# Sums of squares of a graph kernel by block transpose, row sums and small DMAs in place of a product with ones

## The chip, the core and the metric

The kernel runs on one core of a Trainium2 chip. The core has a matrix engine (TensorE, PE in the profile), a vector engine (VectorE, DVE), a scalar engine (ScalarE, ACT), GpSimd (POOL) and SyncE (SP), which here issues all DMAs. Each engine works through its own list of instructions in order, and semaphores hold an instruction back until another engine has done its part. The metric is the device time of one execution in microseconds; lower is better.

## What is computed

128 graphs of 128 nodes with 256 features pass through four layers. Each layer is a graph network with a residual and a layer norm behind it: `x = layernorm(x + layer(x, adj))`. The change lies in the first layer, a hypergraph convolution with a hidden width of 512 and a layer norm of its own over that width:

```python
h = relu(hypergraph_conv(x, adj, W1, b1))
h = layer_norm(h, gamma, beta)          # mean and variance over 512 columns
y = hypergraph_conv(h, adj, W2, b2)
return y + x
...
x = _layernorm(x + _L0_gnn_ref(...))    # then three more layers of this form
```

The variance of the hidden row of a node is its mean of squares less its squared mean. The hidden state is held with the 512 hidden columns along partitions (four chunks of 128) and the nodes along the free axis, so the sum of squares of one node runs over partitions.

## The kernel before

Two graphs make a pair, and 64 pairs are worked off. A pair passes through some forty steps on five engines, and the steps of several pairs are interleaved: a written-out start (`fill`), a loop over `n` from 7 to 61 (`FIRST, LAST = 7, 62`, 55 passes), and a written-out end (`drain`). Each engine has its own `body(n)` that lists its steps in a fixed order. A pass of the loop works on pair `n` in the first steps, on `n-1` in the hidden layer, on `n-2` in the second layer, and so on to `n-5`.

TensorE's pass (`body`, lines 784 to 823) runs `R` (first product of the hidden layer, two halves), `G`, `xT` (transpose of `x1`, the first layer's output, of pair `n-2`), `H2W`, `Ax2`, `XAB`, `H1`, `AP3`, `P` (product of the hidden state with W2 for pair `n-1`), `squares`, `Tr`, `AXB`, `H1W`, `Ax3`, `Gx`, `H2`, `GP` (the product with `p`, which ends layer one of pair `n-1`), `TK`. Products in full precision are split into high and low halves; the low half (`..._lo`) is made by VectorE or GpSimd from a high half (`..._hi`) that ScalarE writes.

The sum of squares of pair `n-1` goes this way. ScalarE squares the hidden state (`square_r`, L1044), GpSimd adds the four chunks to one (`add_squares` L221, `sum_squares` L227, tile `sq1`), and TensorE sums over partitions by two products with a column of ones (`squares`); each fp32 product shows as two matmuls. The result lies in PSUM beside `P`. ScalarE squares the mean (`square_mean` L1091), VectorE makes the variance (`wide_var` L1699 and L1702), ScalarE the root (`root_h` L1095), VectorE the reciprocal and `p` (`make_p` L1709, L1717), ScalarE its high half (`round_p`, `p_hi`), GpSimd its low half (`low_p`, `p_lo`), and TensorE runs `GP`. Behind `GP` VectorE adds the residual (`sum_n1` L1750) and takes moments (`moments(n1)` L1575, L1584), ScalarE the root (`root(n1)` L1005), and VectorE makes `x1` in the next pass (`make_x1` L1595, L1613), which TensorE's `xT` reads.

SP's pass issues the loads of pair `n+2` (`reload`) and the store of pair `n-5`, which waits for the last layer norm. No other DMA runs in the loop.

Of the kernel before, what the change touches and what calls it, by code (L numbers as in the profile page):

```python
# [46 lines left out]
def build(nc, x, adjT, w1T, w2T, wab, v1, v2, v3, wk, columns, rows, eye, out):  # L47
# [5 lines left out]
    with ExitStack() as ctx:  # L53
        def sb(name, shape, dt=F32):
            return ctx.enter_context(nc.sbuf_tensor(name, [C, *shape], dt))
# [4 lines left out]
        def sem(name):  # L60
            return ctx.enter_context(nc.semaphore(name))
# [33 lines left out]
        sq, sq2, sq1 = sb("sq", [KH, 2, C]), sb("sq2", [2, 2, C]), sb("sq1", [2, C])  # L95
        h_mean2 = sb("h_mean2", [2])
        h_veps, h_std, h_rstd = sb("h_veps", [2]), sb("h_std", [2]), sb("h_rstd", [2])
        p_f, p_s = sb("p_f", [2, D]), hi_lo("p", [2, D])
# [25 lines left out]
        class Norm:  # L124
# [13 lines left out]
            def mv(self, p):  # L138
# [11 lines left out]
        table_loaded = sem("table_loaded")  # L150
        consts_step, beta_made, w1_hi, w1_lo, w2_scaled, w2_mean, w2_centred, w2c_hi, w2c_lo = (
            sem(s) for s in ("consts_step", "beta_made", "w1_hi", "w1_lo", "w2_scaled", "w2_mean",
                             "w2_centred", "w2c_hi", "w2c_lo"))
        betaW_made, wab_hi, wab_lo, v_hi, v_lo, b2_made = (
# [5 lines left out]
            sem(s) for s in ("ht_made", "ht_counted", "be_max", "be_made", "be_hi", "be_lo", "bh_high", "bh_made"))  # L160
        dn_0, dn_1, dn_2, dn_3, gl_made, gd_made = (sem(s) for s in ("dn_0", "dn_1", "dn_2", "dn_3", "gl_made", "gd_made"))
# [3 lines left out]
        sq_made, sq_half, sq_sum = sem("sq_made"), sem("sq_half"), sem("sq_sum")  # L165
        hm2, hv, hve, hstd, hrstd = (sem(s) for s in ("h_mean2", "h_var", "h_veps", "h_std", "h_rstd"))
        deg_max, deg_inv = sem("deg_max"), sem("deg_inv")
        p_made, p_hi, p_lo, xb_made = sem("p_made"), sem("p_hi"), sem("p_lo"), sem("xb_made")
# [21 lines left out]
        def bank(stage, pair):  # L190

            return BANK_OF.get((stage, pair), BANK[stage])

        def inputs(p):
# [94 lines left out]
        def _(sp):  # L289
# [80 lines left out]
        def _(pe):  # L370
# [68 lines left out]
            def P(p, h):  # L439
                if p == 0 and h == 0:  # L440
                    pe.wait_ge(w2c_lo, 1)
# [154 lines left out]
            def fill():  # L596
# [10 lines left out]
                pe.wait_ge(gt_hi, 1)  # L607
                pe.wait_ge(w2_mean, 1)
                G(2)
# [174 lines left out]
            def body(n):  # L784
# [22 lines left out]
                P(n - 1, 1)  # L807
                squares(n - 1)
                pe.wait_ge(ax2_lo, n - 2)
# [179 lines left out]
        def _(act):  # L989
# [212 lines left out]
            def round_w2():  # L1202
                act.wait_ge(w2_centred, 1)
                copy(w2c_s[0][:, :, 0:D], w2g[:]).then_inc(w2c_hi, 1)

# [178 lines left out]
            def body(n):  # L1384
# [178 lines left out]
        def _(dve):  # L1563
# [90 lines left out]
            def scale_G(p):  # L1654
# [3 lines left out]
                dve.wait_ge(pe_did["G"], upto(p))  # L1658
                dve.tensor_reduce(dn, psum[:, both, 2 * C:2 * C + 2], AX_X, ALU.add).then_inc(dn_0, 1)
                dve.wait_ge(dn_0, upto(p))  # L1660
                dve.tensor_scalar(dn_max[:], dn, TINY, None, ALU.max).then_inc(dn_1, 1)
                dve.wait_ge(dn_1, upto(p))
                dve.reciprocal(dn_inv[:], dn_max[:]).then_inc(dn_2, 1)
                dve.wait_ge(dn_2, upto(p))
                dve.scalar_tensor_tensor(out=dinv[:], in0=dn, scalar=0.0, in1=dn_inv[:],
                                         op0=ALU.is_gt, op1=ALU.mult).then_inc(dn_3, 1)
                dve.wait_ge(dn_3, upto(p))
                if begun(p - 1):
# [18 lines left out]
            def invert_edges(p):  # L1687
# [5 lines left out]
                dve.reciprocal(be_inv[:], be[:]).then_inc(be_made, 1)  # L1693

            def wide_var(p):
                b = bank("P", p)
                h_var = psum[:, b:b + 2, D + 4]
                dve.wait_ge(hm2, upto(p))
                dve.scalar_tensor_tensor(out=h_var, in0=psum[:, b:b + 2, D + 2], scalar=1.0 / DH,  # L1699
                                         in1=h_mean2[:], op0=ALU.mult, op1=ALU.subtract).then_inc(hv, 1)  # L1700
# [21 lines left out]
            def node_degree(p):  # L1722
                b = bank("AXB", p)
                dve.wait_ge(pe_did["AXB"], upto(p))
                dve.tensor_scalar(degm[:], psum[:, b:b + 2, D], DEG_EPS, None, ALU.max).then_inc(deg_max, 1)
                dve.wait_ge(deg_max, upto(p))
                dve.reciprocal(rdeg[:], degm[:]).then_inc(deg_inv, 1)

            def make_agg(p):
                b = bank("AXB", p)  # L1730
                dve.wait_ge(xa_out, upto(p))
                dve.wait_ge(deg_inv, upto(p))
                for g in range(2):
# [36 lines left out]
            def mean_w2():  # L1770
                dve.wait_ge(pe_did["W2"], 1)
                dve.tensor_scalar(w2mean[:], psum[:, bank("W2", 0), 0:D], 1.0 / DH, None, ALU.mult).then_inc(w2_mean, 1)

            def centre_w2():
                dve.wait_ge(w2_mean, 1)
                dve.wait_ge(w2_scaled, KH)
                dve.tensor_tensor(w2g[:], w2g[:], bc(w2mean[:], [C, KH, D], 1), ALU.subtract).then_inc(w2_centred, 1)

            def high_w2():
                dve.wait_ge(w2_centred, 1)  # L1780
                dve.tensor_copy(w2c_s[0][:, :, 0:D], w2g[:]).then_inc(w2c_hi, 1)

            def low_w2():
                dve.wait_ge(w2c_hi, 1)
                dve.tensor_tensor(w2c_s[1][:, :, 0:D], w2g[:], f(w2c_s[0][:, :, 0:D]),  # L1785
                                  ALU.subtract).then_inc(w2c_lo, 1)

# [198 lines left out]
            def body(n):  # L1986
# [203 lines left out]
        def _(pool):  # L2190
# [121 lines left out]
            def body(n):  # L2312
# [98 lines left out]
```

## Time and profile before

| | us |
|---|---|
| median of three runs | 1393.92 (1392.55 to 1394.46) |
| the profiled execution, device time | 1393.31 |
| its span, first to last instruction | 1391.2 |
| outside the span | 2.1 |

Busy time of the span: TensorE 99%, VectorE 82%, ScalarE 81%, GpSimd 72%; DMA engines a tenth. The chain of work that ended last lies on TensorE for 98% of the span. The granted TensorE clock is 0.997 of full speed on the mean. Times in the rows below are microseconds from the start of the span, if no ns stands beside them; a matmul's end is modelled and matmuls overlap, so the cost of a group of them is read from start to start.

### The profile page before, as it was taken

To read this page: it belongs to the slowest core of one execution; us is meant where nothing else is said; L and a number is where in the kernel's file an instruction comes from. 1 tells how busy PE (TensorE), PEld (TensorE's weight loads), DVE (VectorE), ACT (ScalarE), POOL (GpSimd) and SP (SyncE) were. 2 spreads that over 40 slices of the span, in tenths; PEclk is the share of its full clock that TensorE was granted. 3 is DMA by queue.
4 is the path that set the end of the run, shared out by engine and by line. 5 is a ranking of instruction groups with operands and counts; after the bars stand their busy time and mean duration, and the time that the engine had idled before them with its cause. 6 is when DMAs were issued, how large, how long until landed. Compare 5 with 4: busy or idle time off the path is not lost.

```text
span 1391.2 us, 35333 instructions
## 1 busy us (share of the span) xinstructions
PE 1376.9 (99%) x10946; PEld 1335.9 (96%) x10946; DVE 1134.6 (82%) x4092; ACT 1122.7 (81%) x2639; POOL 1003.6 (72%) x1059
## 2 busy tenths in 40 slices
PE   8999999999999999999999999999999999999997
PEld 8999999999999999999999999999999999999996
DVE  7888788888887887788888878878888888888896
ACT  6777887887888878878878888888788788887776
POOL 5758778778778787787787787777877877877531
PEclk9999999999999999999999999999999999999999
DMA  4100110110100101101101101011011011010000
GB/s 143 36 20 20 40 39 20 39 40 20 39 29 31 39 21 39 39 20 40 39 20 40 32 28 39 21 39 39 21 39 39 20 40 37 23 40 21 8 22 34
DMA packets 29961, 47.17 MB, mean 34 GB/s; under 512 B 3408, under 2 KB 12240, under 8 KB 29776
## 3 DMA queue, kind: packets, MB, share of 16 engines
q1 hardware_dynamic: 29776, 44.91, 10.1%
q8 instruction: 90, 1.47, 0.4%
q14 instruction: 95, 0.78, 0.2%
HBM read 28.12 MB, written 16.78 MB: 32 GB/s over the span
## 4 chain that ended last, share of the span: by engine, by line
PE 98%; ACT 1%; issue 0%; DVE 0%; DMA 0%; SPq 0%; ACTq 0%; DVEq 0%
PE psum L374 95%; PE psum L473 2%; PE psum L417 1%; DMA n_s<-w2T_in 0%; ACT x L1010 0%; ACT tk L1172 0%; ACT h_hi L991 0%; DVE w2c_lo L1785 0%; DVE w2g L1767 0%; ACT w2c_hi L991 0%; ACT r_f L1015 0%; SPq L291 0%; ACT h_f L1015 0%; DVE n_st L1575 0%; DVE n_s L260 0%
## 5 line engine op out<-in xcount | busy, mean ns | idle before, releaser
L208 POOL TENSOR_TENSOR h_lo<-h_f,h_hi 128x512 fp32r<-128x512 f32 x120 | 154.9, 1291 | 93.6 <-ACT h_hi L991 93.4
L1010 ACT ACTIVATE x<-n_s,n_shift,n_rstd 128x256 f32<-128x256 f32 x384 | 208.0, 590 | 4.2 <-DVE n_shift L1599 4.1
L215 POOL TENSOR_TENSOR r_lo<-r_f,r_hi 128x512 fp32r<-128x512 f32 x123 | 158.7, 1292 | 44.1 <-ACT r_hi L991 43.9
L2229 POOL TENSOR_TENSOR n_s<-tk,mask 128x512 f32<-128x512 f32 x60 | 62.5, 1041 | 154.1 <-DVE mask L1652 133.0
L1575 DVE BATCH_NORM_STATS2 n_st<-n_s 128x6 f32<-128x256 f32 x384 | 141.9, 412 | 2.2
L374 PE MATMUL psum<-v_hi,h_hi 128*128 128x256 f32 x512 | 137.8, 292 | 2.0 <-ACT h_hi L991 2.0
L374 PE MATMUL psum<-A_f,x 128*128 128x128 f32 x1024 | 135.5, 275 | 0.6 <-ACT x L1010 0.5
L1015 ACT ACTIVATE h_f<-psum,columns 128x256 f32<-128x256 f32 x256 | 107.6, 472 | 34.8 <-PE psum L374 34.7
L374 PE MATMUL psum<-v_lo,h_hi 128*128 128x256 f32 x512 | 133.3, 282 | 0.0
L374 PE MATMUL psum<-gx_hi,w1T_hi 128*128 128x256 f32 x512 | 132.3, 281 | 0.0
L374 PE MATMUL psum<-gx_hi,w1T_lo 128*128 128x256 f32 x512 | 131.9, 281 | 0.0
L374 PE MATMUL psum<-w2c_hi,r_hi 128*128 128x258 f32 x512 | 129.5, 284 | 0.8 <-DVE w2c_lo L1785 0.8
L374 PE MATMUL psum<-w2c_lo,r_hi 128*128 128x258 f32 x512 | 129.4, 283 | 0.0
L374 PEld LDWEIGHTS psum<-A_f,x 128*128 128x128 f32 x1024 | 124.6, 191 | 1.6 <-ACT x L1010 1.1
L1005 ACT ACTIVATE n_std<-psum,eps_c 128x2 f32<-128x2 f32 x165 | 42.2, 256 | 93.5 <-DVE psum L1584 93.5
L208 DVE TENSOR_TENSOR ax_lo<-psum,ax_hi 128x512 fp32r<-128x512 f32 x128 | 88.5, 692 | 24.3 <-ACT ax_hi L991 21.1
L374 PE MATMUL psum<-wab_hi,x1T_hi 128*128 128x512 f32 x256 | 105.8, 413 | 0.0
L1015 ACT ACTIVATE r_f<-psum,columns 128x256 f32<-128x256 f32 x256 | 100.3, 469 | 5.9 <-PE psum L374 5.0
L374 PE MATMUL psum<-v_hi,h_lo 128*128 128x256 f32 x512 | 102.1, 281 | 0.0
L374 PE MATMUL psum<-gx_lo,w1T_hi 128*128 128x256 f32 x512 | 101.8, 281 | 0.0
L374 PE MATMUL psum<-wab_lo,x1T_hi 128*128 128x512 f32 x256 | 100.9, 394 | 0.0
L208 DVE TENSOR_TENSOR x1T_lo<-psum,x1T_hi 128x512 fp32r<-128x512 f32 x64 | 44.2, 691 | 69.3 <-ACT x1T_hi L991 69.3
(173 smaller groups left out, 5200.1 us busy)
## 6 DMA issues: line engine op xcount, KB each, us to landing
x_in<-x_in_dram SPq DMA_DIRECT2D x64, 256.0 KB, 2.8
out<-x SPq DMA_DIRECT2D x64, 256.0 KB, 2.0
at_in<-adjT SPq DMA_DIRECT2D x64, 128.0 KB, 2.2
x<-v_in SPq DMA_DIRECT2D x3, 256.0 KB, 5.7
n_s<-w2T_in SPq DMA_DIRECT2D x2, 256.0 KB, 3.3
r_f<-w1T_in SPq DMA_DIRECT2D x2, 256.0 KB, 5.1
h_f<-wab_in SPq DMA_DIRECT2D x2, 256.0 KB, 5.6
rows<-rows_in SPq DMA_DIRECT2D x1, 256.0 KB, 6.0
```

The lines of the kernel that those rows point to most:

```text
L208: return e.tensor_tensor(dst[1][:], src, f(dst[0][:]), ALU.subtract).then_inc(signal, 1)
L215: e.tensor_tensor(r_s[1][:, half], r_f[:, half], f(r_s[0][:, half]), ALU.subtract).then_inc(r_lo[h], 1)
L374: return pe.matmul(o, a, b, start=start, stop=stop)
L417: last = pe.transpose(psum[:, bank("Tr", p), cols(g)], Gd[:, g, :], ident[:])
L473: last = pe.transpose(psum[:, bank("xT", p), (2 * m + g) * C:(2 * m + g + 1) * C], x1[p % 2][:, g, cols(m)], ident[:])
L1005: act.activation(nm.std[:], nm.mv(p)[:, :, 1], ACT.Sqrt, bias=eps_c[:, 0:1]).then_inc(nm.rooted, 1)
L1010: last = act.activation(dst[:, g, :], nm.s[:, g, :], ACT.Identity, scale=nm.rstd[:, g:g + 1], bias=nm.shift[:, g:g + 1])
L1015: return act.activation(dst[:, m].rearrange("p g c -> p (g c)"), psum[:, bank(stage, p), (m % 2) * 2 * C:(m % 2 + 1) * 2 * C], ACT.Relu, b ...
L1575: last = dve.bn_stats(nm.st[:, g, :], sum_in_psum(p, g) if nm is n1 else nm.s[:, g, :])
L2229: pool.tensor_tensor(n4.s[:], tk[:], bc(mask[:], [C, 2, D], 2), ALU.mult).then_inc(tk_masked, 1)
```

## The change

In the 55 passes of the loop, the two products with ones are gone, and the sum over partitions is made in four steps: VectorE transposes the 32x32 blocks of `sq1` (`turn_squares`), sums each row of 32 to a partial sum (128x8 values), SP writes these to a small DRAM tensor with four DMAs of 128 runs of 8 bytes each, waits for them, and reads them back with one DMA of 128 rows of 32 bytes (`move_squares`); VectorE adds the four partial sums of each node (`fold_columns`). `wide_var` then reads the sum from SBUF. Pairs outside the loop keep the products with ones.

The orders change with it. TensorE runs `TK` ahead of `GP`. VectorE has `turn_squares` behind `invert_edges`, and `fold_columns` and `wide_var` stand behind `make_agg`, `make_p` behind `sum_n2`. ScalarE has `copy_h1w` ahead of `root_h`, and `high_ax3` between `root_h` and `round_p`. GpSimd has `low_GT`, `make_xb` and `make_x2c` ahead of `low_p`. SP has `move_squares` between `reload` and `store`. Several semaphores are merged into one that counts steps (`w2_step`, `dn_step`, `deg_step`); the waits stay where they were. The core of the diff:

```diff
+        sq_rows = nc.dram_tensor("sq_rows", (C, 4, 2), F32, kind="Internal").ap()
...
         def sum_squares(e, p):
             e.wait_ge(sq_half, upto(p))
             if begun(p - 1):
                 e.wait_ge(pe_did["P"], upto(p - 1))
+            if in_loop(p - 1, 1):
+                e.wait_ge(sq_turned, by_dma(p - 1))
...
+            def move_squares(p):
+                sp.wait_ge(sq_folded, by_dma(p))
+                if in_loop(p - 1, 1):
+                    sp.wait_ge(sq_moved, 16 * by_dma(p - 1))
+                for a in range(4):
+                    sp.dma_start(sq_rows.rearrange("(b i) a g -> a i b g", b=4)[a],
+                                 sq_part[32 * a:32 * a + 32]).then_inc(sq_stored, 16)
+                sp.wait_ge(sq_stored, 64 * by_dma(p))
+                if in_loop(p - 1, 1):
+                    sp.wait_ge(sq_added, by_dma(p - 1))
+                sp.dma_start(sq_cols[:], sq_rows).then_inc(sq_moved, 16)
...
                 if n + 2 < NP:
                     reload(n + 2)
+                if n < LAST:
+                    move_squares(n - 1)
                 store(n - 5)
...
-                    late(o, terms, 1, stop=h == 1)
+                    last = late(o, terms, 1, stop=h == 1)
+                if h == 1 and in_loop(p, 1):
+                    last.then_inc(pe_did["P"], 1)
...
                 P(n - 1, 1)
-                squares(n - 1)
                 pe.wait_ge(ax2_lo, n - 2)
...
                 H2(n - 3)
+                pe.wait_ge(n2.summed, n - 1)
+                TK(n - 4)
                 pe.wait_ge(p_made, n)
                 GP(n - 1)
-                pe.wait_ge(n2.summed, n - 1)
-                TK(n - 4)
...
                 copy_GT(n)
-                root_h(n - 1)
                 round_GT(n)
                 make_x3(n - 4)
+                copy_h1w(n - 3)
+                root_h(n - 1)
+                high_ax3(n - 4)
                 round_p(n - 1)
-                copy_h1w(n - 3)
-                high_ax3(n - 4)
                 high_gx(n)
...
+            def turn_squares(p):
+                dve.wait_ge(sq_sum, upto(p))
...
+                dve.transpose(sq_t[:].rearrange("p g c -> p (g c)"), sq1[:].rearrange("p g c -> p (g c)")).then_inc(sq_turned, 1)
+                dve.wait_ge(sq_turned, by_dma(p))
...
+                dve.tensor_reduce(sq_part[:].rearrange("p b g -> p g b"),
+                                  sq_t[:].rearrange("p g (b j) -> p g b j", b=4), AX_X, ALU.add).then_inc(sq_folded, 1)
+
+            def fold_columns(p):
+                dve.wait_ge(sq_moved, 16 * by_dma(p))
...
+                dve.tensor_reduce(h_sq[:], sq_cols[:].rearrange("p a g -> p g a"), AX_X, ALU.add).then_inc(sq_added, 1)
...
                     invert_edges(n + 1)
+                turn_squares(n - 1)
                 low_xbw(n - 2)
...
-                wide_var(n - 1)
-                make_p(n - 1)
                 node_degree(n - 2)
                 make_agg(n - 2)
+                fold_columns(n - 1)
+                wide_var(n - 1)
                 sum_n2(n - 2)
+                make_p(n - 1)
                 low_ax3(n - 4)
...
+                low_GT(n)
                 make_xb(pool, n - 1)
-                low_GT(n)
+                make_x2c(n - 3)
                 low_p(pool, n - 1)
-                make_x2c(n - 3)
                 low_h2(pool, n - 3)
```

## Rows read from the trace of the kernel before

**Rows 1.** The page's first part: busy us, share, instructions of each engine.
```profile
PE 1376.9 (99%) x10946; PEld 1335.9 (96%) x10946; DVE 1134.6 (82%) x4092; ACT 1122.7 (81%) x2639; POOL 1003.6 (72%) x1059
```

**Rows 2.** Two stretches: length, busy us of each engine, granted clock, DMA share, GB/s.
```profile
170.00:1350.00 1180.00, 1179.94 (x9443) 1148.10 (x9443) 965.48 (x3503) 965.03 (x2270) 885.34 (x925) 1.00 0.10 31
...
1370.00:1380.00 10.00, 7.96 (x63) 7.38 (x62) 8.33 (x36) 6.88 (x16) 0.20 (x1) 1.00 0.08 28
```

**Rows 3.** Chain that ended last, first and last such piece: start, length, work.
```profile
99.80 10.49 PE psum L374 x78
...
1267.60 10.49 PE psum L374 x78
```

**Rows 4.** TensorE in order of time, the products with ones: start, length, work.
```profile
704.40 0.50 PE L374 MATMUL psum<-ones,sq 128*128 128x1 f32 x4
704.76 0.42 PE L417 MATMUL psum<-ident,Gd 128*128 128x128 f32 x2
```

**Rows 5.** DMA issues of the page: KB each, median us to landing.
```profile
x_in<-x_in_dram SPq DMA_DIRECT2D x64, 256.0 KB, 2.8
out<-x SPq DMA_DIRECT2D x64, 256.0 KB, 2.0
...
columns<-columns_in SPq DMA_DIRECT2D x1, 8.0 KB, 1.8
```

**Rows 6.** SP's queue in order of time, one pass's loads being issued.
```profile
713.28 0.33 SPq L291 DMA_DIRECT2D at_in<-adjT  x1
713.66 0.44 SPq L294 DMA_DIRECT2D x_in<-x_in_dram  x1
```

**Rows 7.** VectorE in order of time, from the edge counts to the sum of n2.
```profile
699.88 0.28 DVE L1683 TENSOR_SCALAR HT<-at_in 128x256 fp32r<-128x256 f32 x1
700.20 0.42 DVE L1685 TENSOR_REDUCE ht_count<-HT 128x2 f32<-128x256 f32 x1
...
700.95 0.69 DVE L1640 TENSOR_TENSOR xbw_lo<-psum,xbw_hi 128x512 fp32r<-128x512 f32 x1
...
705.14 0.17 DVE L1699 SCALAR_TENSOR_TENSOR psum<-psum,h_mean 128x2 f32<-128x2 f32 x1
...
705.98 0.88 DVE L1717 SCALAR_TENSOR_TENSOR p_f<-psum,h_rstd,betaW 128x256 f32<-128x256 f32 x2
706.77 0.15 DVE L1725 TENSOR_SCALAR degm<-psum 128x2 f32<-128x2 f32 x1
...
708.14 0.69 DVE L1744 SCALAR_TENSOR_TENSOR n_s<-psum,x 128x512 f32<-128x512 f32 x1
```

**Rows 8.** ScalarE in order of time: p's high half, root of n1, squares.
```profile
706.90 0.62 ACT L991 ACTIVATE p_hi<-p_f 128x512 fp32r<-128x512 f32 x1
...
712.70 0.29 ACT L1005 ACTIVATE n_std<-n_mv,eps_c 128x2 f32<-128x2 f32 x1
...
718.57 1.06 ACT L1044 ACTIVATE sq<-r_f 128x1024 f32<-128x1024 f32 x1
```

**Rows 9.** GpSimd in order of time: p's low half, the last sum of squares.
```profile
707.59 1.28 POOL L208 TENSOR_TENSOR p_lo<-p_f,p_hi 128x512 fp32r<-128x512 f32 x1
...
721.08 0.89 POOL L227 TENSOR_TENSOR sq<-sq 128x256 f32<-128x256 f32 x1
```

**Rows 10.** TensorE in order of time: last matmul of GP, start of R, xT.
```profile
710.43 0.28 PE L374 MATMUL psum<-p_lo,GT_hi 128*128 128x256 f32 x1
...
711.96 0.28 PE L374 MATMUL psum<-gx_hi,w1T_hi 128*128 128x256 f32 x1
...
715.02 0.60 PE L473 MATMUL psum<-ident,x 128*128 128x128 f32 x4
```

**Rows 11.** VectorE in order of time, behind GP: sum of n1, moments, x1.
```profile
710.91 0.67 DVE L1750 SCALAR_TENSOR_TENSOR psum<-xb,psum 128x512 f32<-128x512 f32 x1
...
712.51 0.15 DVE L1584 BATCH_NORM_AGGREGATE n_mv<-n_st 128x2 f32<-128x6 f32 x1
...
713.33 0.99 DVE L1613 TENSOR_SCALAR x<-psum,n_mv,n_rstd 128x256 f32<-128x256 f32 x2
```

More of the change, by code:

```diff
@@ L150, in build @@
         table_loaded = sem("table_loaded")
-        consts_step, beta_made, w1_hi, w1_lo, w2_scaled, w2_mean, w2_centred, w2c_hi, w2c_lo = (
-            sem(s) for s in ("consts_step", "beta_made", "w1_hi", "w1_lo", "w2_scaled", "w2_mean",
-                             "w2_centred", "w2c_hi", "w2c_lo"))
+        consts_step, beta_made, w1_hi, w1_lo, w2_scaled, w2_step = (
+            sem(s) for s in ("consts_step", "beta_made", "w1_hi", "w1_lo", "w2_scaled", "w2_step"))
         betaW_made, wab_hi, wab_lo, v_hi, v_lo, b2_made = (
@@ L160, in build @@
             sem(s) for s in ("ht_made", "ht_counted", "be_max", "be_made", "be_hi", "be_lo", "bh_high", "bh_made"))
-        dn_0, dn_1, dn_2, dn_3, gl_made, gd_made = (sem(s) for s in ("dn_0", "dn_1", "dn_2", "dn_3", "gl_made", "gd_made"))
+        dn_step, dinv_made, gl_made, gd_made = (sem(s) for s in ("dn_step", "dinv_made", "gl_made", "gd_made"))
         w_hi, w_lo, gt_made, gx_hi, gx_lo = (sem(s) for s in ("w_hi", "w_lo", "gt_made", "gx_hi", "gx_lo"))
@@ L165, in build @@
         sq_made, sq_half, sq_sum = sem("sq_made"), sem("sq_half"), sem("sq_sum")
+        sq_turned, sq_folded, sq_stored, sq_moved, sq_added = (
+            sem(s) for s in ("sq_turned", "sq_folded", "sq_stored", "sq_moved", "sq_added"))
         hm2, hv, hve, hstd, hrstd = (sem(s) for s in ("h_mean2", "h_var", "h_veps", "h_std", "h_rstd"))
-        deg_max, deg_inv = sem("deg_max"), sem("deg_inv")
+        deg_step = sem("deg_step")
         p_made, p_hi, p_lo, xb_made = sem("p_made"), sem("p_hi"), sem("p_lo"), sem("xb_made")
@@ L192, in bank, with in_loop, by_dma @@
             return BANK_OF.get((stage, pair), BANK[stage])
+        def in_loop(pair, lag):
+            return FIRST <= pair + lag < LAST
+        def by_dma(pair):
+            return pair - FIRST + 2
         def inputs(p):
@@ L440, in P @@
                 if p == 0 and h == 0:
-                    pe.wait_ge(w2c_lo, 1)
+                    pe.wait_ge(w2_step, 4)
                 outs = [(psum[:, bank("P", p) + g, 0:D + 2],
@@ L607, in fill @@
                 pe.wait_ge(gt_hi, 1)
-                pe.wait_ge(w2_mean, 1)
+                pe.wait_ge(w2_step, 1)
                 G(2)
@@ L1202, in round_w2 @@
             def round_w2():
-                act.wait_ge(w2_centred, 1)
-                copy(w2c_s[0][:, :, 0:D], w2g[:]).then_inc(w2c_hi, 1)
+                act.wait_ge(w2_step, 2)
+                copy(w2c_s[0][:, :, 0:D], w2g[:]).then_inc(w2_step, 1)
             def fill():
@@ L1658, in scale_G @@
                 dve.wait_ge(pe_did["G"], upto(p))
[L1659 to L1664, printed above, removed]
+                dve.tensor_reduce(dn, psum[:, both, 2 * C:2 * C + 2], AX_X, ALU.add).then_inc(dn_step, 1)
+                dve.wait_ge(dn_step, 3 * p + 1)
+                dve.tensor_scalar(dn_max[:], dn, TINY, None, ALU.max).then_inc(dn_step, 1)
+                dve.wait_ge(dn_step, 3 * p + 2)
+                dve.reciprocal(dn_inv[:], dn_max[:]).then_inc(dn_step, 1)
+                dve.wait_ge(dn_step, 3 * p + 3)
                 dve.scalar_tensor_tensor(out=dinv[:], in0=dn, scalar=0.0, in1=dn_inv[:],
-                                         op0=ALU.is_gt, op1=ALU.mult).then_inc(dn_3, 1)
-                dve.wait_ge(dn_3, upto(p))
+                                         op0=ALU.is_gt, op1=ALU.mult).then_inc(dinv_made, 1)
+                dve.wait_ge(dinv_made, upto(p))
                 if begun(p - 1):
@@ L1693, in invert_edges @@
                 dve.reciprocal(be_inv[:], be[:]).then_inc(be_made, 1)
+            def turn_squares(p):
+                dve.wait_ge(sq_sum, upto(p))
+                if in_loop(p - 1, 1):
+                    dve.wait_ge(sq_folded, by_dma(p - 1))
+                dve.transpose(sq_t[:].rearrange("p g c -> p (g c)"), sq1[:].rearrange("p g c -> p (g c)")).then_inc(sq_turned, 1)
+                dve.wait_ge(sq_turned, by_dma(p))
+                if in_loop(p - 1, 1):
+                    dve.wait_ge(sq_stored, 64 * by_dma(p - 1))
+                dve.tensor_reduce(sq_part[:].rearrange("p b g -> p g b"),
+                                  sq_t[:].rearrange("p g (b j) -> p g b j", b=4), AX_X, ALU.add).then_inc(sq_folded, 1)
+            def fold_columns(p):
+                dve.wait_ge(sq_moved, 16 * by_dma(p))
+                if begun(p - 1):
+                    dve.wait_ge(hv, upto(p - 1))
+                dve.tensor_reduce(h_sq[:], sq_cols[:].rearrange("p a g -> p g a"), AX_X, ALU.add).then_inc(sq_added, 1)
             def wide_var(p):
+                if in_loop(p, 1):
+                    dve.wait_ge(sq_added, by_dma(p))
                 b = bank("P", p)
@@ L1698, in wide_var @@
                 dve.wait_ge(hm2, upto(p))
-                dve.scalar_tensor_tensor(out=h_var, in0=psum[:, b:b + 2, D + 2], scalar=1.0 / DH,
+                dve.scalar_tensor_tensor(out=h_var, in0=h_sq[:] if in_loop(p, 1) else psum[:, b:b + 2, D + 2],
+                                         scalar=1.0 / DH,
                                          in1=h_mean2[:], op0=ALU.mult, op1=ALU.subtract).then_inc(hv, 1)
@@ L1724, in node_degree @@
                 dve.wait_ge(pe_did["AXB"], upto(p))
-                dve.tensor_scalar(degm[:], psum[:, b:b + 2, D], DEG_EPS, None, ALU.max).then_inc(deg_max, 1)
-                dve.wait_ge(deg_max, upto(p))
-                dve.reciprocal(rdeg[:], degm[:]).then_inc(deg_inv, 1)
+                dve.tensor_scalar(degm[:], psum[:, b:b + 2, D], DEG_EPS, None, ALU.max).then_inc(deg_step, 1)
+                dve.wait_ge(deg_step, 2 * p + 1)
+                dve.reciprocal(rdeg[:], degm[:]).then_inc(deg_step, 1)
             def make_agg(p):
@@ L1731, in make_agg @@
                 dve.wait_ge(xa_out, upto(p))
-                dve.wait_ge(deg_inv, upto(p))
+                dve.wait_ge(deg_step, 2 * p + 2)
                 for g in range(2):
@@ L1771, in mean_w2 @@
                 dve.wait_ge(pe_did["W2"], 1)
-                dve.tensor_scalar(w2mean[:], psum[:, bank("W2", 0), 0:D], 1.0 / DH, None, ALU.mult).then_inc(w2_mean, 1)
+                dve.tensor_scalar(w2mean[:], psum[:, bank("W2", 0), 0:D], 1.0 / DH, None, ALU.mult).then_inc(w2_step, 1)
             def centre_w2():
-                dve.wait_ge(w2_mean, 1)
+                dve.wait_ge(w2_step, 1)
                 dve.wait_ge(w2_scaled, KH)
-                dve.tensor_tensor(w2g[:], w2g[:], bc(w2mean[:], [C, KH, D], 1), ALU.subtract).then_inc(w2_centred, 1)
+                dve.tensor_tensor(w2g[:], w2g[:], bc(w2mean[:], [C, KH, D], 1), ALU.subtract).then_inc(w2_step, 1)
             def high_w2():
-                dve.wait_ge(w2_centred, 1)
-                dve.tensor_copy(w2c_s[0][:, :, 0:D], w2g[:]).then_inc(w2c_hi, 1)
+                dve.wait_ge(w2_step, 2)
+                dve.tensor_copy(w2c_s[0][:, :, 0:D], w2g[:]).then_inc(w2_step, 1)
             def low_w2():
-                dve.wait_ge(w2c_hi, 1)
+                dve.wait_ge(w2_step, 3)
                 dve.tensor_tensor(w2c_s[1][:, :, 0:D], w2g[:], f(w2c_s[0][:, :, 0:D]),
-                                  ALU.subtract).then_inc(w2c_lo, 1)
+                                  ALU.subtract).then_inc(w2_step, 1)
             def spread_beta():
```

1 line of the change is left out of this document (added).

## The prediction

> **What bounds the kernel now.** I read the page's busy shares first: TensorE is busy 99% of the span, the other engines 72 to 82% [rows 1]. Then the stretches: from 170 to 1350 us TensorE is busy for 1179.94 of 1180 us at a full clock [rows 2]. Nothing in the loop waits for anything but TensorE's own work, and the chain shows the same piece of it from pass to pass, 99.80 us the first and 1267.60 us the last [rows 3]: 1167.8 us over 55 passes are 21.23 us a pass (most are 21.21). So a matmul that goes is a direct gain, as long as the other engines' hand-overs still fit. How much slack these have is the whole question, and it is read from the order of time on each engine in one pass. I use the pass around 700 us; an instant in the next pass is carried back by 21.21.
>
> **What is removed.** The four matmuls with ones start at 704.40, the next step at 704.76 [rows 4]: 0.36 us a pass, 55 passes, 19.8 us. The matmuls' own lengths overlap and are not the price. Alone this would give 1393.3 - 19.8 = 1373.5 us, and TensorE's own work would be 20.85 us a pass.
>
> **What is added, in VectorE.** The last sum of squares ends at 721.08 + 0.89 = 721.97, a pass earlier at 700.76 [rows 9]. VectorE comes to the place of the transpose when it now starts `low_xbw`, at 700.95 [rows 7], 0.2 later; so the transpose waits for nobody. No row shows a transpose. Instructions on 128x256 values take 0.28 (an elementwise one) to 0.42 (a sum along rows), one on 128x512 takes 0.69 [rows 7]; I take 0.42, for the same count of values at the slower rate, with 0.28 and 0.69 as ends. The row sums have a row of their own size, 0.42, and a dependent instruction starts 0.04 after the one ahead (699.88 + 0.28 to 700.20). So the partial sums stand at 700.95 + 0.42 + 0.04 + 0.42 = 701.83, and VectorE's list behind moves by as much.
>
> **What is added, in DMA.** SP is idle then: its loads are issued near 713, where the next pass begins [rows 6]. Issues stand 0.38 apart [rows 6]; four stores need 3 x 0.38 = 1.14 to the last issue. A store of the loop lands 2.0 after its issue, the one small load took 1.8, the slowest kind in the loop 2.8 [rows 5]. With 0.05 for each of three wake-ups the way through DRAM is 1.14 + 2.0 + 1.8 + 0.15 = 5.1 us, and 6.7 with 2.8 at both hops. The stores are of 8-byte runs, which no row shows. The Trainium skill's page DMA: Bandwidth & Descriptors, section Specifications, says that transfers below 512 B make the DMA engine read, modify and write; no run here shows its price, and it would push towards the 6.7. Queued behind SP's waits is only the store of pair n-5, which is due in the next pass, so those waits cost nothing.
>
> **Where VectorE then waits.** `fold_columns` stands behind `low_xbw` to the last shift (700.95 to 705.14, 4.19) and `node_degree` with `make_agg` (706.77 to 708.14, 1.37) [rows 7]: 5.56 us behind the partial sums. The DMAs' 5.1 are hidden by that, with 0.45 to spare; VectorE reaches the fold at about 701.83 + 5.56 = 707.39. If the cover is gone, each 0.1 us counts in each pass.
>
> **From the fold to `GP`.** Fold and the two instructions of `wide_var` are small and dependent, 0.17 and 0.04 each (705.14) [rows 7]: 0.63. Then `sum_n2`, 0.69 and 0.03 [rows 7], under which ScalarE's root is hidden; the reciprocal, 0.21 likewise; `p`, 0.88 [rows 7]. That is 2.44, so `p` stands at 709.83 where it now stands at 706.86. ScalarE's high half is 0.04 + 0.62 [rows 8], GpSimd's low half 0.07 + 1.28 [rows 9]: 711.84. TensorE can have done the first two matmuls of `GP`; four remain, 0.06 + 3 x 0.12 + 0.28 = 0.70, and 0.05 to VectorE: `sum_n1` starts at 712.59, where it started at 710.91 [rows 11]. That is 1.68 late. The sum lays instructions end to end; without a wait between them the next starts some 0.09 early (706.77 against 705.98 + 0.88) [rows 7], at three seams: 1.68 - 0.27 = 1.4.
>
> **Why the delay comes back in every pass.** From `sum_n1` at 710.91 the moments end at 712.66 [rows 11], ScalarE's root of n1 starts at 712.70, and behind it in ScalarE's list, all but back to back, stand ten or so activations, the new pass's hidden state and its squares among them, to 718.57 + 1.06 = 719.63 [rows 8]; then GpSimd's two sums to 721.97 [rows 9]. So the squares of a pair come 11.06 us behind `sum_n1` of the pair before, whatever TensorE does, and the way from the squares to the next `sum_n1` is the sum above: a ring of five engines of 21.21 + 1.4 = 22.6 us, above TensorE's 20.85. In the kernel before, `p` stood at 706.86 and `GP` came when TensorE's list came to it, so the ring had room.
>
> **What is moved.** `TK` ahead of `GP` gives TensorE work while it waits for `p`. Its second half needs `ax3_lo`, which VectorE now makes behind `p`: 709.83 + 0.69 = 710.5, and eight matmuls, 0.95, end at 711.5, before `p_lo`: hidden by 0.3. ScalarE's `root_h` and `round_p` wait now, and `high_gx` is queued behind: high half at 710.49 + 0.6, low half at about 711.8; the next `R` needs it at 712.3, so it is hidden. `make_x2c` ahead of `low_p` ends long before `p` stands. The merged semaphores wait for the same instructions and cost nothing.
>
> **The sum.** 55 x 1.4 = 77, less about 1 because behind the last pass `TK` is already done: 1393.3 + 76 = 1469 us. The profiled execution's 1393.31 lies 0.6 under the median, so against the median it is the same. TensorE would stand idle for about 1.7 us a pass. Its clock should bear that: from 1370 to 1380 us it was busy for 7.96 of 10 us and the granted clock stayed at 1.00 (the 2.4 GHz level) [rows 2].
>
> **Rivals.** First, the DMAs are longer than their cover. At 6.7 the fold comes 6.7 - 5.56 = 1.14 later than VectorE could, a pass is 2.54 longer, 55 x 2.54 - 1 = 139: 1532 us. For it speaks that no 8-byte store is seen; against it, that a store of 256 KB lands in 2.0.
>
> Second, the ring is shorter than I sum, and only the new order bites. Behind the last matmul of `GP` `x1` is ready after 0.33 + 3.41 (710.91 to 713.33 + 0.99) + 0.06 = 3.8 us [rows 11]. `xT`, which reads it, used to come 4.59 behind (710.43 to 715.02). With `TK` gone from between, it is due 0.12 + 3.06 (711.96 to 715.02) = 3.18 behind [rows 10], and waits 0.6. A pass is then 20.85 + 0.6 = 21.45, 0.24 longer: 1393.3 + 13 = 1406 us.
>
> Third, faster: the result comes in time and `xT` does not wait. The mechanism would be that ScalarE and GpSimd, in their new orders, start the hidden state of the next pass earlier than now, so that the ring closes in TensorE's 20.85; it decides at 1.7 us of shortening, and then the gain is 19.8: 1373.5 us. The page just named, section Rules for kernel authors, asks for just this form, a DMA issued early with work behind it and a late wait, so that its fixed cost overlaps; here the DMA is hidden by my sum too, but not the VectorE work that it hides behind. Against it: ScalarE's stretch from the root to the squares shows no room.
>
> **How the numbers follow.** Forecast with hidden DMAs 0.62: 1469, between 1455 (transpose 0.28, and the seams a little better) and 1485 (transpose 0.69). DMAs longer than the cover 0.23: 1475 to 1540. Only `xT` 0.07: 1406. Faster 0.05: 1373.5. Near no change 0.03. "Same" means within 0.2%, about what a measurement of this kernel can tell from no change. Left out of the range are the last three cases and a little at the top, so it reaches from 1425 (a delay of 0.6 a pass) to 1540. Faster 0.05, same 0.03, slower 0.92.
>
> **What would show it.** Passes of about 22.6 us; the matmuls with ones gone from the loop; TensorE idle ahead of `GP` for `p_lo`, and perhaps ahead of `xT` for `x1`; VectorE going into `fold_columns` with little or no idle time; landings of 2 us for the small DMAs. VectorE idle ahead of the fold by more than 0.5 us would make the first rival right. Passes under 21.2 us, with `p_lo` in time, would make the prediction wrong at the step where the ring is closed through ScalarE's order.

## The result, and the profile after

| | before | after |
|---|---|---|
| median, us | 1393.43 | 1515.8 |
| ratio after / before | | 1.0868 (95% interval 1.0839 to 1.0896) |
| profiled execution, device time / span, us | 1393.31 / 1391.2 | 1517.51 / 1515.4 |

One of the four executions after took 6518.07 us, at the full clock, for a reason that is not known; it enters the median but not the ratio, the other three took 1511.56 to 1517.51, and no run of an experiment had the like.

The change costs 122 us, 8.7%. The forecast was 1469 us, in a range of 1425 to 1540: the direction holds, and so does the reason in kind, a ring through several engines that is longer than TensorE's own work. The size is 47 us too low, the ring runs in part through other steps than forecast, and the price of the matmuls that went turned out wrong by more than a factor of five.

From the page of the kernel after, the busy time of each engine (us, share, instructions), and the two DMA groups that are new (KB each, median us to landing):

```profile
PE 1412.6 (93%) x10726; PEld 1323.6 (87%) x10726; DVE 1214.7 (80%) x4257; ACT 1094.0 (72%) x2639; POOL 998.8 (66%) x1059
...
sq_rows<-sq_part SPq DMA_DIRECT2D x220, 1.0 KB, 1.7
sq_cols<-sq_rows SPq DMA_DIRECT2D x55, 4.0 KB, 2.0
```

Against [rows 1] every engine is busy for a smaller share; VectorE's falls least, from 82% to 80%, and it is busy for 80 us more. No engine is the bound by its own work any more. What TensorE, its weight loads (PEld) and VectorE waited for, from 200 to 1340 us and in the whole loop (us in total, times, longest):

```profile
PE psum L401 <- ACT x L1038: 25.4, 49, 0.9
PE psum L502 <- DVE x L1641: 23.9, 48, 0.8
PE psum L401 <- DVE ax_lo L219: 16.8, 25, 0.7
PEld psum L401 <- POOL p_lo L219: 9.7, 49, 0.2
```

```profile
DVE h_sq L1738 <- DMA sq_cols<-sq_rows: 34.1, 33, 1.7
```

In the kernel before TensorE waited for nobody in the loop [rows 2]. Now it waits half a microsecond in each pass for `x3` (first line, ahead of `Ax3`) and for `x1` (second, ahead of `xT`), and in half of the passes for `ax3_lo` in `TK` (and 10.7 us in all for its high half). At `GP` only the weight loads wait, 0.2 us in each pass, for `p_lo`. VectorE waits for the small DMAs in 33 of 55 passes.

The chain of the kernel after, in order of time, over one pass (start, length, work) shows the ring itself: VectorE's fold and `wide_var`, `p`, `ax3_lo`, TensorE's `TK` and `GP`, `sum_n1`, ScalarE's list as far as the high half of `ax2`, VectorE's list from the low half of `ax2` on, the transpose, the row sums, the DMAs.

```profile
759.78 2.04 DMA sq_cols<-sq_rows
...
764.14 0.48 DVE p_f L1765
764.62 0.61 DVE ax_lo L219
765.27 2.19 PE psum L401 x14
767.48 0.71 DVE psum L1798
...
774.38 0.64 ACT ax_hi L1019
775.04 0.69 DVE ax_lo L219
...
778.49 0.46 DVE sq_t L1727
778.96 0.43 DVE sq_part L1731
...
780.73 2.84 DMA sq_rows<-sq_part
783.58 2.10 DMA sq_cols<-sq_rows
```

The squares are not on it. GpSimd's last sum of squares in this pass, in order of time:

```profile
777.48 0.81 POOL L240 TENSOR_TENSOR sq<-sq 128x256 f32<-128x256 f32 x1
```

It ends at 778.29, and VectorE's list comes to the transpose at 778.49, 0.20 us later.

The load through DRAM stands at 759.78 and again at 783.58: a pass of 23.8 us there. Over the loop, first to last such load (131.2 to 1399.1 us, 54 passes), the mean is 23.48; it was 21.23 [rows 3].

The passes come in two kinds. SP's queue, the start of the four stores in two neighbouring passes, twice:

```profile
335.74 1.80 SPq L331 DMA_DIRECT2D sq_rows<-sq_part  x4
...
358.61 1.75 SPq L331 DMA_DIRECT2D sq_rows<-sq_part  x4
...
755.30 1.76 SPq L331 DMA_DIRECT2D sq_rows<-sq_part  x4
...
779.41 1.75 SPq L331 DMA_DIRECT2D sq_rows<-sq_part  x4
```

22.87 us and 24.11 us. What divides them is seen where VectorE reaches the fold. In the short kind, VectorE and GpSimd in order of time:

```profile
340.88 0.15 DVE L1738 TENSOR_REDUCE h_sq<-sq_cols 128x2 f32<-128x8 f32 x1
341.06 0.97 DVE L1746 SCALAR_TENSOR_TENSOR psum<-h_sq,h_mean 128x2 f32<-128x2 f32 x1
```

```profile
340.73 1.27 POOL L253 TENSOR_TENSOR xb<-x_in,b2half 128x512 f32<-128x512 f32 x1
341.96 1.28 POOL L2272 TENSOR_TENSOR x2c<-x,rows 128x512 f32<-128x512 f32 x1
```

And in the long kind:

```profile
761.84 0.16 DVE L1738 TENSOR_REDUCE h_sq<-sq_cols 128x2 f32<-128x8 f32 x1 [1.31 <-DMA sq_cols<-sq_rows]
762.04 0.79 DVE L1746 SCALAR_TENSOR_TENSOR psum<-h_sq,h_mean 128x2 f32<-128x2 f32 x1
```

```profile
761.53 1.27 POOL L2272 TENSOR_TENSOR x2c<-x,rows 128x512 f32<-128x512 f32 x1
```

The first instruction of `wide_var` works on two values a partition and took 0.17 us before [rows 7]. Now it ends when GpSimd's running instruction ends: 341.06 + 0.97 = 342.03 against 340.73 + 1.27 = 342.00, and 762.04 + 0.79 = 762.83 against 761.53 + 1.27 = 762.80. Before, one of its operands lay in PSUM; now both lie in SBUF. If the DMAs come in time it is held to the end of `make_xb`, else to the end of `make_x2c`, 1.24 us later: the 22.87 and the 24.11. So there are three parts to tell apart: the ring, the DMAs, and this hold; and beside them the price of what was removed and of the new orders.

### The profile page after: what moved, and what is told of

It is laid out like the page before. It is cut to its first block, busy times and chain, and to the rows that moved or that the text cites. A ratio compares the mean times of both kernels' runs of the same rounds, so it can differ in the third digit from the quotient of the medians.

```text
span 1515.4 us, 35659 instructions
## 1 busy us (share of the span) xinstructions
PE 1412.6 (93%) x10726; PEld 1323.6 (87%) x10726; DVE 1214.7 (80%) x4257; ACT 1094.0 (72%) x2639; POOL 998.8 (66%) x1059
## 4 chain that ended last, share of the span: by engine, by line
DVE 36%; PE 21%; ACT 15%; issue 13%; DMA 11%; SPq 3%; ACTq 0%; POOL 0%; DVEq 0%; POOLq 0%
PE psum L401 20%; DMA sq_rows<-sq_part 6%; DVE n_st L1603 5%; DVE ax_lo L219 5%; DMA sq_cols<-sq_rows 5%; ACT r_f L1043 4%; ACT x L1038 3%; DVE psum L1746 3%; SPq L331 3%; DVE psum L1798 3%; ACT ax_hi L1019 2%; ACT h2w_hi L1019 2%; DVE p_f L1765 2%; ACT x1T_hi L1019 2%; DVE sq_t L1727 2%
## 5 line engine op out<-in xcount | busy, mean ns | idle before, releaser
L401 PE MATMUL psum<-A_f,x 128*128 128x128 f32 x1024 | 141.5, 282 | 28.7 <-ACT x L1038 28.6
L219 POOL TENSOR_TENSOR p_lo<-p_f,p_hi 128x512 fp32r<-128x512 f32 x59 | 76.4, 1295 | 108.6 <-ACT p_hi L1019 108.5
```

Source lines behind the costliest of these rows:

```text
L219: return e.tensor_tensor(dst[1][:], src, f(dst[0][:]), ALU.subtract).then_inc(signal, 1)
L401: return pe.matmul(o, a, b, start=start, stop=stop)
```

## The experiments

Times are medians in us, ratios against runs of the kernel before on the same chip.

### The hold taken away

`e1_sum_in_psum`, the folded sum written to PSUM:

```diff
+                dve.wait_ge(hm2, upto(p))
-                dve.tensor_reduce(h_sq[:], sq_cols[:]...
+                dve.tensor_reduce(psum[:, bank("P", p):bank("P", p) + 2, D + 2], sq_cols[:]...
-  in0=h_sq[:] if in_loop(p, 1) else psum[:, b:b + 2, D + 2],
+  in0=psum[:, b:b + 2, D + 2],
```

> The changed kernel, but fold_columns writes the folded sum into PSUM, so that wide_var has one operand in SBUF, not two. Theory (a ring through VectorE, the DMAs, ScalarE and GpSimd sets the pass, and wide_var's first instruction, 0.96 us instead of 0.17 in the changed kernel, is held until GpSimd's running instruction ends because both its operands lie in SBUF): that instruction is back at about 0.17, a pass is 0.76 us shorter, 55 x 0.76 = 42, 1515.8 - 42 = 1474 us (1465 to 1485). Rival (the time beyond the forecast is all from the small DMAs, and the long instruction merely fills a wait that is there anyway): 1515 us, unchanged.

Measured 1485.92, ratio 1.0675 (1.0659 to 1.0691): 30 us less than the kernel after, not 42, and 1 us outside the expected range. VectorE's groups kept apart by shape (busy us, mean ns), `wide_var` and the fold in this run:

```profile
L1747 DVE SCALAR_TENSOR_TENSOR psum<-psum,h_mean 128x2 f32<-128x2 f32 x64 | 10.7, 167 | 2.4 <-ACT h_mean L1119 0.5
...
L1739 DVE TENSOR_REDUCE psum<-sq_cols 128x2 f32<-128x8 f32 x55 | 9.2, 167 | 36.4 <-DMA sq_cols<-sq_rows 36.3
```

The instruction is back at 167 ns and the rival (nothing changes) falls. The DMA waits stay, 36.3 us.

### The DMAs taken away

`e2_no_dram` folds what lies in `sq_part` at hand; `e3_no_dram_psum` does so and writes to PSUM.

```diff
-                if n < LAST:
-                    move_squares(n - 1)
-                dve.wait_ge(sq_moved, 16 * by_dma(p))
+                dve.wait_ge(sq_folded, by_dma(p))
-                dve.tensor_reduce(h_sq[:], sq_cols[:]...
+                dve.tensor_reduce(h_sq[:], sq_part[:]...
```

> The changed kernel without the way through DRAM: fold_columns adds what lies in sq_part, so the sums over the other three blocks are left out and the values are not the reference's. Theory: every pass takes what the short passes of the changed kernel take, 22.87 us (those in which the DMAs came in time, with wide_var held): 1393.3 + 55 x (22.87 - 21.23) - 1 = 1482 us. Rival (DMAs alone are what the forecast had too low): 1469 us, the forecast with hidden DMAs. Rival (only the waits for DMA make it slower at all): below 1394 us.

> Both edits: no way through DRAM (three of four blocks left out of the sum) and the folded sum in PSUM. Theory: the ring alone, 22.87 - 0.76 = 22.1 us a pass: 1393.3 + 55 x 0.87 - 1 = 1440 us (1430 to 1450), still well above the kernel before although neither a DMA nor a held instruction is left. Rival (the ring is no bound by itself, the two stalls are everything): 1374 to 1407 us.

Measured: `e2_no_dram` 1484.62 (1.0673, 1.0657 to 1.0688), `e3_no_dram_psum` 1450.98 (1.0426, 1.0408 to 1.0443). In `e2_no_dram` every pass is of the short kind; `wide_var` in two passes in order of time:

```profile
706.06 0.97 DVE L1744 SCALAR_TENSOR_TENSOR psum<-h_sq,h_mean 128x2 f32<-128x2 f32 x1
...
728.93 0.97 DVE L1744 SCALAR_TENSOR_TENSOR psum<-h_sq,h_mean 128x2 f32<-128x2 f32 x1
```

22.87 us apart, as expected. With the hold gone as well, `e3_no_dram_psum` has (1449.1 - 1391.2) / 55 + 21.23 = 22.28 us a pass without either stall, and the time is 4.3% above the kernel before and 1 us above the expected range. The hold is worth 0.59 a pass, not the 0.76 by which the instruction is shorter, because another way binds below it. The chain of `e3_no_dram_psum` no longer passes through fold, `wide_var` and `p`; it leaves VectorE's list ahead of them, through the moments of n3 and n4 to ScalarE's `x3`, and then lies on TensorE from `Ax3` to `GP` (start, length, work):

```profile
728.62 0.46 DVE sq_t L1725
...
729.44 0.68 DVE xbw_lo L1666
...
733.73 0.98 ACT x L1036 x2
...
734.76 5.09 PE psum L399 x42
739.87 0.71 DVE psum L1797
```

And `p_lo` now stands ahead of its use. GpSimd making it, and TensorE's first weight load of it:

```profile
715.33 1.30 POOL L219 TENSOR_TENSOR p_lo<-p_f,p_hi 128x512 fp32r<-128x512 f32 x1 [0.52 <-ACT p_hi L1017]
716.83 0.19 PEld L399 LDWEIGHTS psum<-p_lo,GT_hi 128*128 128x128 f32 x1
```

It is ready at 716.63, 0.20 us early; from 200 to 1340 us the weight loads wait for `x3` and `x1` alone. So in this run the new sums cost time not by the way that their result takes, but because transpose and row sums put off all that stands behind them in VectorE's list, by 0.82 us in the pass shown (728.62 to 729.44), and `x3` with it. That is read from the trace: no run moved `turn_squares` behind the moments, or made `x3` earlier in the changed kernel.

### Which half of the way through DRAM

`e7_rows_out` stores whole rows of 32 bytes and leaves the 8-byte runs to the loads:

```diff
-                for a in range(4):
-                    sp.dma_start(sq_rows.rearrange("(b i) a g -> a i b g", b=4)[a], sq_part[32 * a:32 * a + 32])...
+                sp.dma_start(sq_rows, sq_part[:]).then_inc(sq_stored, 16)
...
-                sp.dma_start(sq_cols[:], sq_rows).then_inc(sq_moved, 16)
+                for b in range(4):
+                    sp.dma_start(sq_cols[32 * b:32 * b + 32], sq_rows.rearrange("(a i) b g -> b i a g", a=4)[b])...
```

> The changed kernel with the small runs on the other side: one store of 128 rows of 32 bytes, then four loads that pick 8-byte runs. Theory A (the scattered landing of the four stores, 1.4 to 4.1 us, comes from writing 8-byte runs to DRAM): the DMAs come in time in nearly all passes, 22.87 us a pass, 1482 us. Theory B (scatter comes with any DMA of this size and number, or reads of 8 bytes scatter as well): 1505 to 1525 us.

Measured 1486.76 (1.0669, 1.0655 to 1.0684), as without DRAM within 2 us. From its DMA view (issues, KB each, median us to landing):

```profile
sq_cols<-sq_rows SPq DMA_DIRECT2D x220, 1.0 KB, 1.7
sq_rows<-sq_part SPq DMA_DIRECT2D x55, 4.0 KB, 1.4
```

The number of DMAs and the bytes are the same, and now they come in time: VectorE's wait ahead of the fold is 4.3 us in the loop where it was 34.1. The four small stores had landed 1.4 to 4.1 us after issue; the four small loads land after 1.5 to 3.3. The row transfer is shorter too, a median of 1.4 as a store and 2.0 as a load. So the form with 8-byte stores and a row load is what came late; how much of the gain belongs to either of the two transfers was not taken apart.

`e9_rows_out_psum` puts this and `e1_sum_in_psum` together:

> The changed kernel with both stalls mended and the sum complete: one store of 32-byte rows and four loads, and the folded sum in PSUM. Theory (two stalls, and under them a ring of 22.3 us): as without DRAM and with PSUM, 1451 us, within 6. Rival (DMAs become the bound again as soon as wide_var is short): 1465 us or more.

Measured 1455.25 (1.044, 1.0426 to 1.0454). The two stalls together are 60.6 us of the 122, and both can be mended. No run mended the rest; the chain of this one is that of `e3_no_dram_psum`, through `x3`.

### The orders alone, and TK's place

`e5_orders_only`: the kernel after without transpose, sums and DMAs, and with `squares(n - 1)` back behind `P` in TensorE's list.

> All the orders of the changed kernel (TK ahead of GP, make_p behind sum_n2, and so on), but the sums of squares by TensorE as before, without transpose, row sums and DMAs. Theory: TensorE's own work is 21.21 us again, and xT waits for x1 for some 0.5 us because TK no longer lies between GP and xT; 21.7 us a pass, 1393.3 + 55 x 0.5 = 1420 us (1410 to 1430). Rival (the orders are free and only the new way of the sum costs): 1393 us.

Measured 1428.35 (1.0251, 1.0236 to 1.0267). The only wait of TensorE in it is at `xT`; two passes in order of time:

```profile
710.34 0.66 PE L496 MATMUL psum<-ident,x 128*128 128x128 f32 x4 [0.47 <-DVE x L1636]
...
732.19 0.66 PE L496 MATMUL psum<-ident,x 128*128 128x128 f32 x4 [0.46 <-DVE x L1636]
```

21.85 us a pass with a wait of 0.47 us. So the orders alone cost 35 us; 24 of them, counted from 200 to 1340 us, are this wait, which is there because `TK` no longer lies between `GP` and `xT`, and the rest was not traced. This 35 is not a share of the 122: in the kernel after the same wait lies inside a longer ring.

`e6_gp_first` is the kernel after with TensorE's old order:

```diff
-                pe.wait_ge(n2.summed, n - 1)
-                TK(n - 4)
                 pe.wait_ge(p_made, n)
                 GP(n - 1)
+                pe.wait_ge(n2.summed, n - 1)
+                TK(n - 4)
```

> The changed kernel with TensorE's old order, GP ahead of TK. Theory: the ring runs through ScalarE's activations behind the root of n1 and not through TensorE's xT, so the place of TK matters little: 1515 us, within 15. Rival (the wait of xT for x1 that TK's new place opened is what makes the pass longer): 0.5 us a pass less, 1488 us.

Measured 1587.7 (1.1387, 1.1363 to 1.1412): 72 us more, and both expectations missed. TensorE's waits in it:

```profile
PE psum L401 <- DVE p_f L1765: 59.2, 46, 2.4
PE psum L401 <- POOL p_lo L219: 37.5, 46, 0.8
```

TensorE sits idle for `p` with `TK` still to do, and does `TK`, `R`, `G`, `xT` behind it; ScalarE has `high_x1T`, which needs `xT`, ahead of `round_r` in its list. So the ring has a second strand, through TensorE. How much it costs is read from single passes, from store to store (length, busy us of TensorE, weight loads, VectorE, ScalarE and GpSimd, granted clock, DMA share, GB/s):

```profile
222.51:245.69 23.18, 21.45 (x169) 20.34 (x168) 18.79 (x67) 17.04 (x42) 16.31 (x18) 1.00 0.11 30
245.69:272.86 27.17, 24.20 (x169) 23.09 (x168) 18.09 (x67) 17.36 (x42) 16.28 (x18) 0.87 0.09 26
...
1062.10:1086.59 24.49, 21.53 (x169) 20.42 (x168) 18.97 (x67) 17.08 (x42) 16.29 (x18) 1.00 0.10 28
```

At the full clock a pass takes 23.2 to 23.3 or 24.49 us, where the kernel after has 22.87 and 24.11: 0.3 to 0.4 us more, some 20 us over 55 passes (an estimate). The passes with a lower clock, 28 of the 54 between two stores, take 24.7 to 27.2 us and hold the larger part of the 72 (last section). So a move that is bad in the old kernel helps in the new one, and most of what undoing it cost goes with the lower clock.

### What the removed matmuls were worth

`e4_no_squares` is the kernel before with `squares(n - 1)` deleted from the loop and the sums of squares left out.

```diff
                 P(n - 1, 1)
-                squares(n - 1)
```

> The kernel before with the products with ones taken out of the loop and nothing in their place; the variance is made from the sum's column, so the sums of squares are left out. Price of what was removed. Theory: 0.36 us a pass, 55 x 0.36 = 19.8: 1373.5 us. Rival (four matmuls of one column cost only what lies beyond the neighbours' overlap, 0.1 us a pass): 1388 us.

Measured 1388.39 (0.998, 0.9971 to 0.9989): 3 us, not 20. The rival's time came out, but not its cause, as `e10_no_squares_x3` shows below. TensorE's weight loads waited for one thing in it, and its chain shows the same (start, length, work):

```profile
PEld psum L374 <- ACT x L1011: 15.2, 51, 0.6
```

```profile
700.09 0.70 DVE n_s L1761
...
704.25 1.10 ACT x L1011 x2
...
705.39 8.04 PE psum L374 x68
```

From the end of `AP3` (700.07) VectorE adds, takes the moments of n3 and n4, ScalarE copies `GT` twice and then makes `x3`, and `Ax3` starts at 705.39. TensorE's `P`, `squares`, `Tr`, `AXB`, `H1W` lie beside that stretch, and it is nearly as long as they were. In the kernel before it was covered, but only just. ScalarE's `x3` there, and the first weight load of `Ax3`, which needs it:

```profile
705.91 1.08 ACT L1010 ACTIVATE x<-n_s,n_shift,n_rstd 128x256 f32<-128x256 f32 x2
...
707.05 0.97 PEld L374 LDWEIGHTS psum<-A_f,x 128*128 128x128 f32 x8
```

`x3` is ready at 706.99, 0.06 us before the weight load; over 55 passes that is 3.3 us, about what the deletion gave.

`e10_no_squares_x3` makes `x3` earlier in the same kernel, and `e12_x3_alone` does that to the kernel before with all its matmuls:

```diff
                 square_mean(n - 1)
+                make_x3(n - 4)
+                root_h(n - 1)
                 copy_GT(n)
-                root_h(n - 1)
                 round_GT(n)
-                make_x3(n - 4)
...
                 wide_var(n - 1)
+                node_degree(n - 2)
                 make_p(n - 1)
-                node_degree(n - 2)
```

> The kernel before without the products with ones (sums of squares left out, as in the run without squares), and with x3 made earlier: ScalarE has make_x3 ahead of copy_GT, root_h and round_GT, VectorE node_degree ahead of make_p. Theory (taking the four matmuls away gave 3 us instead of 20 because the way from AP3 through VectorE's moments of n3 and ScalarE's make_x3 to Ax3 is as long as TensorE's work beside it): with x3 about 1 us earlier the gain comes through, 1375 us (1372 to 1380). Rival (four one-column matmuls are just worth 3 us): 1388 us.

> The kernel before with nothing but the earlier x3 (make_x3 ahead of root_h, copy_GT and round_GT on ScalarE, node_degree ahead of make_p on VectorE); all products with ones stay. Theory: TensorE has no idle time in the loop before, so the order alone gives nothing: 1393 us, within 3, and the gains of the two runs with it come from the matmuls. Rival (the order itself is the gain, since the run without squares and with it lost 24.6 us where 19.8 were worked out): 1388 us.

Measured: `e10_no_squares_x3` 1368.67 (0.9825, 0.9812 to 0.9839), `e12_x3_alone` 1392.6 (0.9992, 0.9983 to 1.0001). The order alone gives nothing measurable, the deletion alone 3 us, both together 24.6, which is 3 us below the expected range. The matmuls are worth their 0.36 us and a little more (24.6 / 55 = 0.45; the other 0.09 was not traced), but only once the stretch beside them is shortened.

### A version that is faster than both

The sum can stay on TensorE at a lower price: `e8_one_pass` takes `sq1` and the ones in the one-pass format, two matmuls instead of four, and `e11_one_pass_x3` adds the earlier `x3`.

```diff
-  sq1 = sb("sq1", [2, C])
+  sq1 = sb("sq1", [2, C], F32R)
+  ones_r = sb("ones_r", [2], F32R)
-  mm(psum[:, bank("P", p) + g, D + 2:D + 3], sq1[:, g, :], ones[:, 0:1], True, True)
+  mm(psum[:, bank("P", p) + g, D + 2:D + 4], sq1[:, g, :], ones_r[:], True, True)
```

> The kernel before in all its orders, but the products with ones take sq1 and the ones in the one-pass fp32 format (float32r, which rounds sq1), two columns wide: two matmuls a pass where there were four. Theory: TensorE's work is the bound there, 0.18 us a pass less, 64 passes with the ends: 1393.3 - 11 = 1382 us. Rival (a one-pass matmul of two columns takes as long as the two-pass one): 1393 us.

> A whole kernel: the one-pass products with ones (0.14 us from their start to the next step, where the two-pass ones take 0.36) and x3 made earlier as in the run beside it. Theory: 0.22 us a pass come through, 55 x 0.22 = 12: 1381 us (1378 to 1386). Rival: 1392 us, as the one-pass products alone.

Measured: `e8_one_pass` 1392.54 (0.9992, 0.9983 to 1.0), `e11_one_pass_x3` 1383.14 (0.9925, 0.9912 to 0.9937). TensorE in order of time in the latter:

```profile
698.56 0.28 PE L375 MATMUL psum<-ones_r,sq 128*128 128x2 f32 x2
698.70 0.44 PE L418 MATMUL psum<-ident,Gd 128*128 128x128 f32 x2
```

0.14 us from the products to the next step, where [rows 4] have 0.36. The 0.22 us a pass are 12 us; 10 arrive. Alone, the cheaper products gave no more than 0.6 us, for the same reason as the deletion. For `e8_one_pass` the expectation named the wrong cause: its rival (one pass costs as much as two) gives the right time, but the rows show the shorter products; the gain was lost in the stretch to `x3` (in its trace `x3` is ready at 705.69 and the first weight load of `Ax3` starts at 705.74).

## Why the prediction was right, and where it was off

- **The ring.** Right in kind, and in part wrong in its members. A loop through several engines sets the pass, and it does come back from `sum_n1` through ScalarE's list. But it does not close through the squares and GpSimd's two sums, as the step on the delay that comes back has it: the chain goes from ScalarE's high half of `ax2` through VectorE's own list to the transpose, and the squares were ready 0.20 us before. Between `p` and `GP` the forecast's way through `p_lo` and the one through `ax3_lo` and `TK`, which it called hidden by 0.3, end within 0.2 us of each other. The sign "TensorE idle ahead of `GP` for `p_lo`" showed only in the weight loads; TensorE's idle time lies ahead of `Ax3`, `xT` and `TK`.
- **VectorE's list.** The step "VectorE's list behind moves by as much" was followed to the fold and no further. Ahead of the fold in that list stand the moments from which `x3` is made, and `x3` had 0.06 us of room. Without either stall this is what the pass of 22.28 us by `e3_no_dram_psum` rests on, and `p_lo` is ready 0.20 us early there. That the number is near the forecast's 22.6 is luck.
- **Transpose and row sums.** Taken as 0.42 each; 0.44 and 0.42 measured.
- **The way through DRAM.** The term that was mis-sized first. The four issues stand 0.38 and twice 0.47 apart instead of 0.38, and the slowest of the four stores lands up to 4.1 us after its issue, where 2.0 was taken: from the first store's issue to the load's it takes 2.83 to 5.40 us, 3.72 in the median, where the sum has 3.19. From the partial sums at 755.28 to the fold at 761.84 it was 6.56 us, not 5.1. In 33 passes VectorE's 5.56 us of work did not hide it: 34.1 us of idle time. So the main case, hidden DMAs at 0.62, failed in these passes, and the first rival, at 0.23, names the reason. `e7_rows_out` shows that it is this form of the transfer and not the number of DMAs or bytes. The Trainium skill's page DMA: Bandwidth & Descriptors, section Specifications, named there, says that transfers below 512 B are read, modified and written. The uneven landing times don't show that mechanism, and 8-byte loads land unevenly too.
- **`wide_var`.** The step "fold and the two instructions of `wide_var` are small and dependent, 0.17 and 0.04 each" failed. It took the duration of an instruction with one operand in PSUM for one with both in SBUF; the median is 0.96. The Trainium skill's page SBUF — State Buffer, section SBUF: two separate sides, states that VectorE with two SBUF inputs and a GpSimd instruction that reads SBUF exclude each other for the whole instruction. The rows agree to 0.03 us, and `e1_sum_in_psum` takes the effect away. That page bore on the sum and was not weighed.
- **What is removed.** The step "a matmul that goes is a direct gain" and its 1373.5 us were wrong for this list: 1388.39 by `e4_no_squares`. A TensorE that never waits only shows that nothing is later than it, not by how much. `x3` stood at 706.99 and the first weight load of `Ax3` at 707.05 in the pass that the prediction read: 0.06 us of room, and a reader of [rows 2] alone does not see it. It did not decide the forecast, since the ring lies above.
- **The rivals.** The second one, `xT` waiting for `x1`, is real: 0.47 us where 0.6 was worked out. In the kernel after it is a wait inside a longer ring. No rival named the hold of `wide_var` or the delay of `x3`.
- **The clock.** Right for the kernel after: 1.00 in each stretch from 200 to 1340 us with TensorE 92 to 94% busy.

Why the sum came near all the same: the ring was laid 14 us too long (1469 against 1455.25 with both stalls mended), and the two stalls added 60.6 us. The top of the range, 1540, was laid for DMAs longer than their cover; about half of the 60.6 us is the hold, which was not thought of, so that the time lies inside the range is in part luck.

## What to carry to other kernels

An engine that is busy all the time is the bound, but the gain of taking work from it is capped by the shortest room of the hand-overs that lie beside that work; read the instant at which each operand is ready against the instant at which it is used, before counting a deleted instruction as a gain. Work that leaves the bounding engine goes into the list of another, and there it puts off everything that stands behind it, not only its own result; the loop through these hand-overs can overtake the engine's own work though each of its members has idle time. So follow every hand-over behind the new work, here `x3` as well as the sum. When an operand moves from PSUM to SBUF, look at what GpSimd runs at that moment.

## What the runs showed of the hardware that was not expected

- A VectorE instruction on 128x2 values with both inputs in SBUF took 0.33 to 1.31 us beside GpSimd's 128x512 additions, and ended 0.02 to 0.04 us behind their end in 44 passes of the kernel after; with one input in PSUM it took 0.167 us (`e1_sum_in_psum`).
- Four DMAs of 128 stores of 8 bytes to DRAM land unevenly, 1.4 to 4.1 us after issue; one of 128 rows of 32 bytes has a median of 1.4, and four of 128 loads of 8 bytes land after 1.5 to 3.3.
- In `e6_gp_first` the granted clock fell in the loop. A stretch of 5 us of it (length, busy us of TensorE, weight loads, VectorE, ScalarE and GpSimd, granted clock, DMA share, GB/s):

```profile
800.00:805.00 5.00, 5.00 (x35) 5.00 (x35) 3.68 (x16) 3.07 (x7) 1.36 (x2) 0.75 0.42 131
```

Between the levels of 2.4 and 1.2 GHz a mean of 0.75 says that half of the stretch ran at the lower. Ahead of it TensorE had waited 0.74 us for `p`, done two matmuls and waited 0.83 us more. The mean over the whole run was 0.960, against 0.998 in the kernel after. When it falls is not told by these waits alone: in the pass ahead TensorE waited 0.70 and 0.83 us at the same two places, and the clock stayed at 1.00.
